# Up-projections of one 128-feature tile by 512 tokens, down-projection sums in two PSUM banks, in a fused fp32r transformer block on TensorE

## What is computed

```python
def ffn(x):                      # 256 -> 1024 -> 256, one of 8 low-rank experts per token
    top1 = argmax(softmax(x @ gate_W.T + gate_b))
    base = x @ wi_W.T + wi_b
    # for the expert i that a token chose:
    return relu(base + (x @ lora_A[i].T) @ lora_B[i].T) @ wo_W.T + wo_b

def attn(x):                     # an xLSTM layer and a gated layer
    h = rmsnorm(x) * ln1_w
    q, k, v = h @ wq, h @ wk, h @ wv             # 16 heads of 16
    i, f = exp(clip(h @ wi + bi, -10, 10)), sigmoid(h @ wf + bf)
    C = f * C + i * outer(v, k); n = f * n + i * k      # token by token, per head
    x = x + (C @ q / max(abs(n . q), 1)) @ wo
    h2 = rmsnorm(x) * ln2_w
    return x + (silu(h2 @ w_gate) * (h2 @ w_up)) @ w_down     # 256 -> 704 -> 256

x = x + 0.5 * ffn(layernorm(x))
x = x + attn(layernorm(x))
x = x + 0.5 * ffn(layernorm(x))
```

## Time and profile before

| | us |
|---|---|
| median of three runs (900.94 to 910.37) | 904.32 |
| span of the profiled execution | 900.5 |
| TensorE busy, instructions | 844.4 (94%), 12744 |
| TensorE weight loads busy | 811.9 (90%) |
| VectorE busy | 622.3 (69%) |
| ScalarE busy | 359.0 (40%) |
| GpSimd busy | 249.6 (28%) |

### The profile page before, as it was taken

One profiled execution on the slowest core, in us unless ns is written; L12 is line 12 of the kernel. 1 busy time (PEld: TensorE's weight loads), 2 busy tenths in 40 slices (PEclk: granted clock), 3 DMA queues, 4 the chain that ended last, 5 costly groups with the idle time before them and its releaser, 6 DMA issues.

```text
span 900.5 us, 30800 instructions
## 1 busy us (share of the span) xinstructions
PE 844.4 (94%) x12744; PEld 811.9 (90%) x12744; DVE 622.3 (69%) x1502; ACT 359.0 (40%) x716; POOL 249.6 (28%) x234
## 2 busy tenths in 40 slices
PE   3958899999899999999899999999999989999998
PEld 3958889999899998999799998899989979899998
DVE  6546795685857777576777868668585898697642
ACT  5453262434425353343523436244452462234421
POOL 2022343130442133221223224313044133612100
PEclk9989999999999999999999999999999999999999
DMA  9214535102434023402324302621043145510000
GB/s 249 84 35 119 158 98 161 54 26 61 116 116 109 13 64 100 131 27 65 85 77 134 96 24 70 176 80 53 9 116 114 42 126 134 158 47 2 1 25 24
DMA packets 66313, 76.04 MB, mean 84 GB/s; under 512 B 12702, under 2 KB 48670, under 8 KB 66176
## 3 DMA queue, kind: packets, MB, share of 16 engines
q1 hardware_dynamic: 66176, 74.09, 29.5%
HBM read 56.75 MB, written 17.30 MB: 82 GB/s over the span
## 4 chain that ended last, share of the span: by engine, by line
PE 77%; issue 6%; DVE 6%; SPq 4%; ACT 2%; POOL 2%; DMA 2%; ACTq 0%; POOLq 0%; DVEq 0%
PE bank L1092 22%; PE bank L1094 20%; PE bank L1093 20%; PE bank L1127 3%; SPq L437 3%; PE bank L1250 2%; PE bank L1310 2%; PE bank L1289 1%; PE bank L1329 1%; PE bank L1264 1%; PE bank L1344 1%; DMA parts_scratch<-pc 1%; DMA dm<-f_scratch 1%; PE bank L1270 1%; POOL pc L555 1%
## 5 line engine op out<-in xcount | busy, mean ns | idle before, releaser
L643 ACT ACTIVATE r_h<-bank 128x512 fp32r<-128x512 f32 x128 | 76.5, 598 | 232.1 <-PE bank L1127 175.3
L1092 PE MATMUL bank<-xT_hi,wi_hi 128*128 128x256 f32 x512 | 146.6, 286 | 1.7 <-DVE r_l L835 1.2
L1092 PE MATMUL bank<-wo_hi,r_h 128*128 128x256 f32 x512 | 146.2, 286 | 0.2
L1094 PE MATMUL bank<-xT_lo,wi_hi 128*128 128x256 f32 x512 | 143.7, 281 | 0.0
L1094 PE MATMUL bank<-wo_lo,r_h 128*128 128x256 f32 x512 | 143.7, 281 | 0.0
L1093 PE MATMUL bank<-wo_hi,r_l 128*128 128x256 f32 x512 | 143.7, 281 | 0.0
L1093 PE MATMUL bank<-xT_hi,wi_lo 128*128 128x256 f32 x512 | 143.5, 280 | 0.0
L835 DVE SCALAR_TENSOR_TENSOR r_l<-bank,r_h 128x512 fp32r<-128x512 f32 x128 | 87.6, 685 | 75.9 <-ACT r_h L643 75.7
L1092 PE MATMUL bank<-xT_hi,wgu_hi 128*128 128x256 f32 x352 | 101.7, 289 | 0.0
L1092 PEld LDWEIGHTS bank<-xT_hi,wi_hi 128*128 128x128 f32 x512 | 96.8, 189 | 3.6 <-DVE vq L915 1.7
L1094 PE MATMUL bank<-xT_lo,wgu_hi 128*128 128x256 f32 x352 | 98.3, 279 | 0.0
(11 more groups left out here) (157 smaller groups left out, 2114.2 us busy)
## 6 DMA issues: line engine op xcount, KB each, us to landing
dm<-f_scratch SPq DMA_DIRECT2D x128, 128.0 KB, 2.9
arena<-parts_scratch SPq DMA_DIRECT2D x96, 128.0 KB
arena<-parts_scratch SPq DMA_DIRECT2D x96, 64.0 KB
arena<-parts_scratch SPq DMA_DIRECT2D x32, 192.0 KB
x<-in_x SPq DMA_DIRECT2D x16, 256.0 KB, 3.1
parts_scratch<-pa SPq DMA_DIRECT2D x64, 64.0 KB
parts_scratch<-pb SPq DMA_DIRECT2D x64, 64.0 KB
parts_scratch<-pc SPq DMA_DIRECT2D x64, 64.0 KB
```

The source lines that it names most:

```text
L643: nc.scalar.activation(flat(r_h[:, n]), U[use % 2][:], ACT.Relu).then_inc(f_rh, 1)
L1092: nc.tensor.matmul(dst, lh, rh, start=first, stop=False, **more)
L1094: return nc.tensor.matmul(dst, lh, rl, start=False, stop=last, **more)
```

## The change

1. **Up-projections.** xT is stored as 512 tokens per 128 features, not by halves. A slot of runs 1 and 2 is one feature tile by 512 tokens: 6 matmuls of 512 columns and one low-rank one. In run L a use holds one gate tile or one up tile; the last use has the last 64 gate and 64 up features in one. There are 11 uses in place of 12. All wait for both halves of xT.
2. **Down-projections.** A slot is one feature tile for all four token tiles: the same 12 matmuls of 256 columns, two products into T0 and two into T1. The sums of both halves are complete after the last slot; the two final additions are a stream of their own, F. The first V of a run waits for T0's addition before its first two products, and for T1's before the other two.
3. **Scores.** T1 takes a bank that was S1. The scores have one bank and wait for the product of the unit before (a_P n in place of n - 1).
4. **Order.** The strings of all five engines are new. TensorE's has 432 U in place of 440 and as many of the others; VectorE's has the letter F.

The diff, cut:

```diff
-L_TILES = tuple(((2 * p * P, (2 * p + 1) * P), (UP_AT + 2 * p * P, UP_AT + (2 * p + 1) * P)) for p in range(IT // 2 - 1)
-                ) + (((I_FULL - P, REST_AT), (UP_AT + I_FULL - P,)),)
+L_TILES = tuple((p * P, UP_AT + p * P) for p in range(IT - 1)) + ((REST_AT,),)
+L_USES = sum(len(tiles) for tiles in L_TILES)
...
 ORDER = {
     "PE": """
-        3G U G 5U 2V 4U 2V 4U 2V 2U 2V 2G 5U G U 2G 2U G 8U V U V 3U 2V 2U 2S Y U V 3U V U 2V 2M S M Y S Y G Y S M G 5U 2M U S Y U M G Y U S Y S M G M U M Y G
...
+        3G U G 6U 2V 2U V U V 3U V 2U V U 2V 2G 6U 2G 2U 2G 8U V 2U V 2U V S 4U Y S V U V 2U 2V 3M V S 2Y S M Y S G 2M G 2U S M 2U Y U Y U S M Y G M U S U Y M
...
-        xT_h, xT_l = pair("xT", [P, 2, 2, DC, HALF])
+        xT_h, xT_l = pair("xT", [P, 2, DC, BLOCK])
...
-        U0, U1, T, G, S0, S1, M, W = (ctx.enter_context(nc.psum_tensor(f"bank{n}", [P, 512], F32)) for n in range(8))
-        U, S = (U0, U1), (S0, S1)
+        U0, U1, T0, G, S, T1, M, W = (ctx.enter_context(nc.psum_tensor(f"bank{n}", [P, 512], F32)) for n in range(8))
+        U, T = (U0, U1), (T0, T1)
...
+            def F_():
+                for r in RUN:
+                    if r.kind == "A":
+                        continue
                     xb = x[:, r.b % XBUFS]
                     for h in range(2):
...
                         to = flat(xb[:, 2 * h:2 * h + 2])
-                        dve.wait_ge(f_dn, r.slot + (h + 1) * r.pairs)
+                        dve.wait_ge(f_dn, r.slot + r.tiles)
                         if r.ffn:
                             dve.wait_ge(g_xb, r.k + 1)
-                            v.scalar_tensor_tensor(to, T[:], 0.5, to, ALU.mult, ALU.add).then_inc(f_fin, 1)
+                            v.scalar_tensor_tensor(to, T[h][:], 0.5, to, ALU.mult, ALU.add).then_inc(f_fin, 1)
...
-                                pe.wait_ge(g_lo, 2 * r.i + h + 1)
+                                pe.wait_ge(g_lo, 2 * r.i + 2)
...
-                                for q in range(2):
-                                    cols = slice((2 * p + q) * P, (2 * p + q + 1) * P)
-                                    dst = U[use % 2][:, q * HALF:(q + 1) * HALF]
-                                    for c in range(DC):
-                                        product(dst, (wi_h[:, c, cols], wi_l[:, c, cols]), (xT_h[:, n, h, c], xT_l[:, n, h, c]),
-                                                q == 0 and c == 0, False, skip_group_check=True)
+                                for c in range(DC):
+                                    product(U[use % 2][:], (wi_h[:, c, cols], wi_l[:, c, cols]), (xT_h[:, n, c], xT_l[:, n, c]), c == 0, False)
...
-                                    done = nc.tensor.matmul(dst, lora_b[0:LS2, cols], u_st[0:LS2, h * HALF:(h + 1) * HALF],
-                                                            start=False, stop=True, skip_group_check=True)
-                                done.then_inc(f_up, 1)
+                                nc.tensor.matmul(U[use % 2][:], lora_b[0:LS2, cols], u_st[0:LS2], start=False, stop=True).then_inc(f_up, 1)
...
-                        if p == 0:
-                            pe.wait_ge(f_fin, 2 * r.d + h)
...
+                        for j in range(TILES):
+                            h, jj = divmod(j, 2)
+                            if s == 0 and jj == 0 and r.d:
+                                pe.wait_ge(f_fin, 2 * r.d - 1 + h)
+                            t, dst = slice(j * P, (j + 1) * P), T[h][:, jj * D:(jj + 1) * D]
...
-                        if n > 1:
-                            pe.wait_ge(a_P, n - 1)
+                        if n:
+                            pe.wait_ge(a_P, n)
```

More of the change, by code:

```diff
@@ L83, in __init__ @@
         self.use = sum(USES[kind] for kind in before)
-        self.slot = sum(2 * PAIRS[kind] for kind in before)
-        self.pairs = PAIRS[self.kind]
+        self.slot = sum(SLOTS_OF[kind] for kind in before)
+        self.tiles = SLOTS_OF[self.kind]
 RUN = [Run(i) for i in range(len(RUNS))]
@@ L347, in n_ml, with of_half @@
         def n_ml(l, s):
-            halves, p = divmod(s, IT // 2)
-            return (2 * l + halves) * (IT // 2 + 1) + (p + 1 if p < IT // 2 - 1 else IT // 2 + 1)
+            return IT * l + s + 1
+        def of_half(t, n, h):
+            return t[:, n, :, h * HALF:(h + 1) * HALF]
         def by_half(t):
@@ L635, in R_ @@
                         yield from projections(r)
-                    for s in range(2 * r.pairs):
+                    for s in range(r.tiles):
                         slot, n = r.slot + s, (r.slot + s) % 2
@@ L642, in R_ @@
                                 act.wait_ge(f_dn, slot - 1)
[L643 removed]
+                            nc.scalar.activation(r_h[:, n], U[use % 2][:], ACT.Relu).then_inc(f_rh, 1)
                             yield
                         else:
[L646 removed]
+                            use, ls = r.use + 2 * s, IT * r.l + s
+                            rows = slice(0, P if s < IT - 1 else REST)
                             act.wait_ge(f_up, use + 1)
@@ L1099, in U_ @@
                     if r.ffn:
-                        begun = [(s, part) for s in range(2 * r.pairs) for part in range(2)]
+                        begun = [(s, part) for s in range(FT) for part in range(2)]
                         if r.k == 0:
@@ L1207, in V_ @@
                 for r in RUN:
-                    for s in range(2 * r.pairs):
-                        h, p = divmod(s, r.pairs)
+                    for s in range(r.tiles):
                         slot, n = r.slot + s, (r.slot + s) % 2
@@ L1288, in S_ @@
                                 own = slice(q // 2 * TH, (q // 2 + 1) * TH)
-                                done = nc.tensor.matmul(S[n % 2][tile, i * TH:(i + 1) * TH], ks[:, j % 2, h, tile], qs[:, j % 2, h, own],
+                                done = nc.tensor.matmul(S[tile, i * TH:(i + 1) * TH], ks[:, j % 2, h, tile], qs[:, j % 2, h, own],
                                                         start=True, stop=True)
```

229 lines of the change are left out of this document (105 added, 124 removed).

## The result

The changed kernel takes **924.31 us** (median of 4 runs, 920.31 to 926.09) against 905.48 for the kernel before. The ratio is 1.0204, with a 95% interval of 1.0159 to 1.0249: it is slower, by about 2%. The forecast was 903, the upper end of its range 919. The profiled execution spans 924.0 us against 900.5. These two are not typical. In the other runs the time is 2.1 to 2.2 us above the span, so the profiled execution before took some 902.6 us, near the fast end of its kernel, and the changed one is the slowest of its four (926.09). The profiles lie 23.5 us apart, the medians 18.8.

What follows compares the result with a forecast made beforehand. TensorE's stream was taken to bound the kernel from about 100 us on. Span 900.5 - 11.0 + 4.5 + 1.4 + 1.4 + 2.0 + 0.7 = 899.5 us, with 3.8 carried over to the median: 903 us, range 884 to 919.

Steps and rivals of the forecast that it cites:

- What bounds the kernel: Whole kernel: from about 100 us on, TensorE's stream sets the time, and what other engines gain is worth nothing.
- The stream: Up-projections: 1424 matmuls of 512 columns replace 2848 narrower ones, saving 7.7 ns a pair, 11.0 us less.
- the third of my cases: Up-projection matmuls: the addition is a share of the width, 233.4 ns at 512 columns, so the change saves nothing.
- The order: TensorE's order: more passages between big and small units, 29 x 0.09 + 19 x 0.10 = 4.5 us more.
- Start: After the first run: 1.4 us more for doubled additions and statistics, 1.4 us more for second-block transposes side by side.
- Up-projections wait for both halves: TensorE idle before up-projections: 1.6 us in the last gated layer, 0.4 in the fifth, 2 us more.
- SyncE's load: Early load of block 2, moved behind the first block's parts: costed at nothing, about 3 us if late.
- End: Last sums on VectorE before the store: two addition steps in place of one, 0.7 us more.
- No saving by width: Rival on up-projection matmuls: the addition is a share of the width, giving 914 us; chance 0.15.
- The one bank of the scores: Rival: 64 score units wait for VectorE's product, 0.3 us each, 19 us, giving 922; chance 0.15.
- My own marks of error: Wrong if TensorE's busy time outside the start falls below 96% of a stretch, or 512-wide distance leaves 223 to 233.

Runs made afterwards that it cites:

- e10: Kernel before with 128 extra 32-column matmuls in TensorE's idle time at 47 us; 926.04 us, ratio 1.0230.
- e11: Kernel before with 32 extra 32-column matmuls in TensorE's idle time at 47 us; 916.52 us, ratio 1.0117.
- e4: Kernel before with 88 extra 240-column matmuls, read by nothing, in TensorE's waits of the first 77 us; 915.69 us, ratio 1.0117.
- e14: Kernel before, but only the feed-forward runs' up-projections wait for both halves, order unchanged; 906.44 us, ratio 1.0006.
- e3: Changed kernel with 108 extra 240-column matmuls, read by nothing, where TensorE waits between 45 and 77 us; 914.83 us, ratio 1.0110.
- e2: Changed kernel, but SyncE loads block 2's x right after its weight loads, as the kernel before does; 921.44 us, ratio 1.0172.
- e13: Kernel before, but only the gated layers' up-projections wait for both halves, with 50 places in the orders moved; 924.37 us, ratio 1.0211.
- e5: Kernel before, but every up-projection waits for both halves, with 50 places in the orders moved; 928.70 us, ratio 1.0239.
- e15: Kernel before with 128 extra matmuls in waits of the fill, lengthening TensorE's program by one packet of 256 instructions; 904.28 us, ratio 0.9975.

## Why the prediction was wrong, by its steps

**What bounds the kernel.** Right as to TensorE's stream. Incomplete in two ways: I read the list of waits past the issue waits, and took the clock as given. Both are worth more than most terms of my sum: issue waits 5.9 to 8 us, the clock up to 7.

**The stream, -11.0.** Here the first step failed. I took the addition as lying between one per instruction (223.3 ns) and one that grows as from 256 to 288 columns (228.1), and set it at 225.7. Measured are 234 ns, the third of my cases, the share of the width. e10 and e11 show why 256 columns gain nothing from widening: past the first one, a 32-column matmul of this kind takes (3.39 - 0.26) / 28 = 112 ns from start to start, and a 240-column one of e4 (4.64 - 0.28) / 39 = 112 as well. Under 256 columns something that does not depend on the width sets the pace, and at 256 the columns have caught up with it (117). It follows the clock: at the half level, in e10, it is (19.36 - 0.26) / 89 = 215 ns by the row, and 213 between single starts in the trace. The rows, all cut behind the first matmul, are from e11, e4 and e10:

```profile
46.45 3.39 PE L1098 MATMUL bank<-wi_hi 128*128 128x32 f32 x29
46.37 4.64 PE L1098 MATMUL bank<-wi_hi 128*128 128x240 f32 x40
50.77 19.36 PE L1098 MATMUL bank<-wi_hi 128*128 128x32 f32 x90
```

The Trainium skill, in "TensorE: Matmul & The Clock Gate", section "LDWEIGHTS (loading the stationary operand)", gives a weight load the time of its columns over 1.2 GHz, 107 ns for 128. The floor of 112 ns lies 5 ns above it, at the full clock; the 213 ns at the half clock do not fit it. Had I put the 107 ns beside the 106.7 ns of 256 columns, it would have said that the loads were already hidden. That the load is what sets the floor fits these numbers; no run isolates it.

**The order, +4.5.** Not isolated. From run L.0 to L.4, where the fill is over, the changed kernel loses 3.0 us more, in a stretch in which the other has 4.8 us of issue waits that the changed order avoids. So the passages and all else that the change costs there come to some 8 us, an estimate, and the shorter rows, which the same passages make, may pay most of it back. I had counted only one side.

**Start, +1.4 and +1.4.** The first is right: the additions and statistics take 1.29 + 1.40 us where they took 0.69 + 0.75, and the first idle is 6.39 us, within the forecast 5.3 to 6.7.

```profile
47.50 1.29 DVE L876 SCALAR_TENSOR_TENSOR x<-bank,x 128x512 f32<-128x512 f32 x2 [0.26 <-PE bank L1097]
48.71 1.40 DVE L931 BATCH_NORM_STATS2 a_st<-x 128x6 f32<-128x256 f32 x4
...
53.85 1.12 PE L1238 MATMUL bank<-ident,xn 128*128 128x128 f32 x4 [6.39 <-ACT xn L733]
```

The second, for all the rest of the fill, is the great miss: 17 us are lost between the profiles' runs 1.0 and L.0, and some 13 when e14's profile stands for the kernel before (an estimate). e3 gives back 5.0 by run L.0 (it stands at +13.3 there) and 9.5 over the whole; e2 gives back 3.6 by run L.0. Two profiles of one time differ by as much as that, so these shares are rough.

**Up-projections wait for both halves, +2.0.** This step failed in kind, not only in size. I asked how long TensorE would stand between the transposes and the first up-projection *in the new order*, and found 1.6 us in the last layer and 0.4 in the fifth. The trace has just that: one wait of 1.5 us, in the last layer at 842 us. What I left out is what the first half's up-projections had been covering: they were the work that TensorE did while the second half was added, normalised and transposed. Taken away with the order hardly touched, they cost 18 to 19 us in the gated layers (e13), all of them behind run L.0. The redrawn order must cover this in the steady part, as the changed kernel loses next to nothing there; other blocks' work can do it. In the fill and at the end fewer blocks are at hand, and there the changed kernel's loss lies. For the end this fits e13, whose profile loses 6.0 us over its last two gated layers. For the fill it is not shown: up to run L.0, e5, e13 and e14 stand 6.0, 5.0 and 3.5 us behind, and e15, which has no such wait, 4.3. So in the old order the wait costs next to nothing there, and no run takes it out of the changed kernel. After the filling, 10 to 12 us of the change are left (e3 against e15), and how they divide between the cover, the sums that complete only with a run's last slot, and the late loads stays open.

**SyncE's load, at nothing.** I named its price should it be late, about 3 us for one load of 256 KB. It was late, with the 512 KB of a block, and e2 gives 2.9, within its noise. The decay matrix behind it waited 2.6 us longer.

**End, +0.7.** Two additions in 1.29 us in place of one of 0.69: right.

**The rivals.** "No saving by width" is true as to its mechanism; its 914 lacked the fill. "The one bank of the scores" gives nearly the right time, 922, for a wrong reason: no wait of the scores for the product is in the list. My own marks of error both fired: TensorE busy 94.14 of 100 us between 700 and 800, and a distance past 233 ns. The first was badly set, though, as the kernel before has 95.33 there, already below my 96%.

## What to carry to other kernels

When a change makes work wait for a later input, don't price the new wait alone: list what the freed work was covering, and look for where nothing else can cover it, as at the end here. Read the waits called issue before comparing two kernels: with long rows of short matmuls they moved by 8 us when the program grew by 64 instructions (e11), so an experiment that adds instructions should add a whole packet's worth, 256 here. Look at the clock of all runs before reading it off one profile: here the profiled execution had the highest of 41. And a wider fp32r matmul is only worth its trouble below the width at which its columns reach the floor, some 245 here, an estimate from 112 ns and 234/512 ns a column.

## What the runs showed of the hardware

- **Issue waits** of TensorE, 0.2 to 3.4 us each, sit at one place of every 256 instructions of its program (100 of 102 in 18 traces). They come back at the same matmuls with 256 instructions added, and at others with 64 or 128: 5.9 and 7.6 us against 14.1 and 16.5.
- **fp32r matmuls by width**, with a 128x128 weight load each, from start to start at the full clock: 32 columns 112 ns, 240 112, 256 117, 288 132, 512 234. At the half clock: 32 columns 213, 288 240.
- **The clock.** In e4 TensorE waited from 511.5 to 514.65 us, and the stretch behind has 0.50 (first fence below). In e10 TensorE worked on 32-column matmuls from 46.3 to 70 us with no wait; the half level came at 50.1 us and stayed until 77.4. With 240-column ones in the same place, the clock was full from 45 to 65 us (e10, then e4).
- **One kernel's clock** differs from execution to execution: 0.979 to 0.992 over 41 runs of the kernel before.

```profile
514.65:517.00 2.35, 2.35 (x34) 2.16 (x34) 0.00 (x0) 0.00 (x0) 0.72 (x1) 0.50 0.92 248
```

```profile
50.00:77.00 27.00, 25.51 (x119) 25.14 (x119) 3.43 (x14) 4.85 (x11) 0.27 (x2) 0.50 0.00 1
```

```profile
45.00:65.00 20.00, 17.97 (x142) 16.59 (x142) 9.18 (x30) 10.94 (x27) 4.11 (x4) 1.00 0.12 35
```
